# A fused attention and FFN kernel: row maxima by PSUM bank in a ring of four, weighted sums in bursts of two tiles

## What is computed

```python
# x: (8, 512, 1024) f32; mask = cond_2048: (8, 1024) of 0 and 1; 16 heads of 32 channels
Q, K, V = (einsum('oc,bct->bto', W, x) for W in (Wq, Wk, Wv))
att = einsum('bhqd,bhkd->bhqk', Q, K) / sqrt(32) + b
att = att * m + (1 - m) * -1e30
att = softmax(att)
y = einsum('bhqk,bhkd->bhqd', att, V)          # back to (8, 512, 1024)
absmax = max(|y|) over the last axis (1024); scale = max(absmax, 1e-7) / 127
q = clip(round(y / scale), -128, 127).astype(int8)
acc = einsum('bsk,nk->bsn', q, weight)          # int8 weight 1024 x 1024
out = x + (acc * scale * w_scale + bias).astype(float16)
```

## Time and profile before

| | us |
|---|---|
| median of 3 runs (lowest, highest) | 2414.74 (2414.34, 2416.75) |
| the profiled execution, its own time | 2414.74 |
| its span, first to last instruction | 2412.8 |
| TensorE busy | 2342.3 (97%) |
| GpSimd busy | 1725.1 (71%) |
| VectorE busy | 1561.4 (65%) |
| ScalarE busy | 1343.3 (56%) |

### The profile page before, as it was taken

How to read it: one execution, slowest core, us unless ns; L and a number is a source line. 1 busy time by engine, 2 the same in 40 slices (tenths; PEclk the granted TensorE clock), 3 DMA queues, 4 the chain that set the end, 5 groups by cost and what they waited for, 6 DMA issues and landing times.

```text
span 2412.8 us, 36511 instructions
## 1 busy us (share of the span) xinstructions
PE 2342.3 (97%) x11840; PEld 1320.4 (55%) x11872; DVE 1561.4 (65%) x1683; ACT 1343.3 (56%) x2536; POOL 1725.1 (71%) x740
## 2 busy tenths in 40 slices
PE   8999999999999999999999999999999999999996
PEld 7888888885444444444444444444444444444442
DVE  3311111147787777777787877777778777787771
ACT  3322222215666666666666666666666666666664
POOL 3322233324888888888888888888888888888887
PEclk9999999999999999999999999999999999999998
DMA  6645554467888888898988998888988888989971
GB/s 244 255 187 216 200 200 184 175 213 165 194 185 194 193 191 199 195 195 196 203 194 191 195 194 193 190 188 191 196 195 184 197 190 195 201 193 194 204 151 47
DMA packets 152569, 462.60 MB, mean 192 GB/s; under 512 B 15592, under 2 KB 51432, under 8 KB 128304
## 3 DMA queue, kind: packets, MB, share of 16 engines
q0 software_dynamic: 27216, 198.19, 42.9%
q10 hardware_dynamic: 48864, 129.19, 20.5%
q1 hardware_dynamic: 76416, 134.34, 15.5%
HBM read 161.51 MB, written 100.93 MB: 109 GB/s over the span
## 4 chain that ended last, share of the span: by engine, by line
PE 77%; DMA 10%; POOL 5%; issue 3%; ACT 2%; ACTq 1%; SPq 1%; DVE 1%; POOLq 0%; DVEq 0%
PE score L725 18%; PE pv L754 16%; PE ring L131 15%; PE ring L324 11%; PE score L324 9%; DMA q_stack<-max_lo 8%; PE ring L788 4%; POOL acc L1026 4%; PE pv L324 3%; PE ring L769 1%; ACT probs L836 1%; DMA k_stack<-bias_part 1%; ACTq L119 1%; DMA probs<-probs 1%; PE ring L779 1%
## 5 line engine op out<-in xcount | busy, mean ns | idle before, releaser
L836 ACT ACTIVATE probs<-score 128x512 f32<-128x512 f32 x2048 | 1076.8, 604 | 590.6 <-PE score L725 539.8
L140 DVE TENSOR_REDUCE neg_max<-ring 128x1 f32<-128x1024 f32 x1024 | 1210.8, 1220 | 260.3 <-PE ring L131 251.8
L725 PE MATMUL score<-q_stack,k_stack 100*128 100x512 f32 x2048 | 878.1, 430 | 36.4 <-DMA q_stack<-max_lo 21.1
L1026 POOL TENSOR_TENSOR acc<-acc,probs 128x2048 f32<-128x2048 f32 x189 | 876.8, 4639 | 21.5 <-DMA probs<-probs 12.9
L131 PE MATMUL ring<-k_stack,q_stack 98*128 98x512 f32 x2048 | 811.4, 396 | 2.8 <-DMA k_stack<-bias_part 1.8
L725 PEld LDWEIGHTS score<-q_stack,k_stack 100*128 100x128 f32 x2048 | 386.1, 189 | 530.1 <-ACT probs L836 370.9
L754 PE MATMUL pv<-probs,v_in 128*32 128x512 f32 x4096 | 546.3, 605 | 0.0
L131 PEld LDWEIGHTS ring<-k_stack,q_stack 98*128 98x128 f32 x2048 | 389.3, 190 | 73.4 <-DVE neg_max L140 6.8
L1026 POOL TENSOR_TENSOR acc<-probs 128x2048 f32<-128x2048 f32 x63 | 288.7, 4582 | 191.5 <-DMA probs<-probs 121.9
L526 POOL TENSOR_TENSOR q_stack<-x_raw,k_stack 128x1024 fp32r<-128x1024 f32 x28 | 67.7, 2455 | 292.2 <-ACT k_stack L402 292.2
L1010 POOL DMA_DIRECT2D probs<-probs x189 | 172.8, 914 | 52.2 <-PE pv L754 48.8
(11 more groups left out here) (101 smaller groups left out, 1950.0 us busy)
## 6 DMA issues: line engine op xcount, KB each, us to landing
probs<-probs POOLq DMA_DIRECT2D x189, 1024.0 KB, 9.1
q_stack<-qk_part ACTq DMA_DIRECT2D x183, 256.0 KB, 7.9
k_stack<-qk_part ACTq DMA_DIRECT2D x90, 512.0 KB
qk_part<-part_hi SPq DMA_DIRECT2D x64, 512.0 KB, 2.6
qk_part<-part_lo SPq DMA_DIRECT2D x64, 512.0 KB, 3.5
v_steps<-v_out SPq DMA_DIRECT2D x64, 256.0 KB, 2.2
v_out<-x ACTq DMA_DIRECT2D x32, 512.0 KB, 5.6
out<-v_out SPq DMA_DIRECT2D x64, 256.0 KB, 2.0
```

What stands on the lines that cost most here:

```text
L140: nc.vector.tensor_reduce(neg_max[:, pair // CHUNK, pair % CHUNK:pair % CHUNK + 1], ring[:, :], AX_X, ALU.max, negate=True).then_inc(neg_m ...
L725: pe.matmul(score[score_bank(t)][:, :], k_stack[par][0:ROWS, h, kt * P:(kt + 1) * P], q_stack[par][0:ROWS, half, h, :], start=True, stop=T ...
L836: nc.scalar.activation(probs[:, kt, h, :], score[score_bank(t)][:, :], ACT.Exp).then_inc(exp_done, 1)
L1026: nc.gpsimd.tensor_tensor(acc[:, half, :, :], first, probs[:, tile, :, :], ALU.add).then_inc(acc_done, 1)
```

## The change

The maxima are taken per PSUM bank: VectorE makes 64 maxima of 128x512 in a step, and the ring is four single banks. A new operation, `join_max`, takes the smaller of the two negated half maxima for a chunk, twice over, so that the transposed chunk holds both parts' rows and one DMA stores both. `weigh` runs for two tiles at t % 8 = 3. The extras move to t = 19 (transposed maxima), 27 (sums), 51 (transposed maxima), 55 (`turn_q`), 59 (sums and FFN); each takes one bank. ScalarE rounds in two operations of 128x1024. All loads of `attend` go from ScalarE's queue to SP's. GpSimd's pairs are tiles 0 to 1, 4 to 5 and 6 to 7, its additions 1 + 2, 3, 5, 7, and its order in a step is new; bias and residual come one step later. The last step has an order of its own: a fourth bank for scores once the maxima are done, the second half's sums by TensorE from five tiles and two pairs' results, VectorE and ScalarE sharing the rounding, and no extra pass. Cut to its core:

```diff
 RING = 8
-PAIRS_OF_TILES = ((0, 1), (2, 3), (6, 5))
-FIRST, ADDED = 4, (1, 3, 7, 5)
+PAIRS_OF_TILES = ((0, 1), (4, 5), (6, 7))
...
+OWN = 18
 EARLY = (UNITS - OWN) // 2
-SUMS_1, TURN_Q, FFN, SUMS_0 = 23, 47, 51, 55
-EXTRAS = (SUMS_1, TURN_Q, FFN, SUMS_0)
-USES = [use for t in range(1, UNITS, 2) for use in ((("max", t), ("extra", t)) if t in EXTRAS else (("max", t),))]
+HALVES = 2 * PAIRS
+BURST = 2 * GH
+RINGS = 4
+TURN_1, SUMS_1, TURN_0, TURN_Q, SUMS_0 = 19, 27, 51, 55, 59
+FFN, SKEW = SUMS_0, SUMS_1
+EXTRAS = {TURN_1: ("turn",), SUMS_1: ("sums",), TURN_0: ("turn",), TURN_Q: ("turn_q",),
+          SUMS_0: ("unused", "sums", "ffn0", "ffn1")}
...
+def reduce_max(nc, dve, bank, half_max, s, pair, half, rowmax_done, neg_max_done):
+    dve.wait_ge(rowmax_done, HALVES * s + 2 * pair + half + 1)
+    nc.vector.tensor_reduce(half_max[:, pair // CHUNK, pair % CHUNK, half:half + 1], bank[:, :],
                             AX_X, ALU.max, negate=True).then_inc(neg_max_done, 1)
...
+def join_max(nc, dve, half_max, neg_max, s, chunk, neg_max_done, joined):
+    dve.wait_ge(neg_max_done, HALVES * s + 2 * CHUNK * (chunk + 1))
+    nc.vector.tensor_reduce(neg_max[:, chunk, :].rearrange("p (d c) -> p d c", d=2),
+                            half_max[:, chunk, :, :].rearrange("p (o c) k -> p o c k", o=1).to_broadcast([P, 2, CHUNK, 2]),
+                            AX_X, ALU.min).then_inc(joined, 1)
...
+def store_max(sp, q_stack, max_parts, par, chunk, max_rows):
+    dst = q_stack[par][ROW_MAX:ROW_MAX + 2, chunk, :, :]
+    sp.dma_start(dst.bitcast(F32), max_parts[:, chunk, :].bitcast(F32)).then_inc(max_rows[chunk], 16)
...
+            def step(s, par, prev=True, ahead=True):
+                first = isinstance(s, int) and s == 0
+                second = not isinstance(s, int) or s >= 2
+                if ahead and not first:
+                    sp.wait_ge(score_done, UNITS * s)
+                    for k in range(3):
+                        load_k(sp, qk_d, k_stack, s + 1, 1 - par, k, k_loaded)
+                    for part in range(2):
+                        load_bias(sp, bias_d, k_stack, s + 1, 1 - par, part, k_loaded)
+                if second:
+                    store_out(s - 2, 0)
                 if ahead:
...
+                    if first:
+                        for i in range(2):
+                            sp.wait_ge(v_stored[i], 16 * B * TT // 2)
+                    wait(sp, pv_done, QH * TT * s)
+                    sp.dma_start(v_in[:, 1 - par, :, :], v_d[bass.ds(s + 1, 1)].rearrange("o p a c -> (o p) a c")).then_inc(v_loaded[1 - par], 16)
+                sp.wait_ge(max_lo_done, 2 * s + 2)
+                store_max(sp, q_stack, max_parts, par, 1, max_rows)
+                if ahead:
+                    for k in range(3):
+                        load_q(sp, qk_d, q_stack, s + 1, 1 - par, 1, k, q2_loaded)
+                if second:
+                    store_out(s - 2, 1)
+                    sp.wait_ge(out_stored, 32 * (s - 1))
+                if prev:
+                    sp.dma_start(res[:, :], x[bass.ds((s - 1) * P, P), :]).then_inc(res_loaded, 16)
+                if ahead:
                     sp.wait_ge(max_lo_done, 2 * s + 3)
...
+                    store_max(sp, q_stack, max_parts, 1 - par, 0, max_rows)
+                if not isinstance(s, int) or s + 2 < STEPS:
...
+                    for k in range(3):
+                        load_q(sp, qk_d, q_stack, s + 2, par, 0, k, q1_loaded)
             sp.wait_ge(proj_done, PROJECTED)
...
+            def step(s, par, prev=True, ahead=True):
                 for t in range(UNITS):
...
+                    scores(s, par, t)
+                    if has_max(t, ahead):
                         next_max(s, par, t)
                     if t == GH - 1 and prev:
...
+                        for kt in (QH * TT - 2, QH * TT - 1):
+                            weigh(s - 1, 1 - par, kt)
+                    if t % BURST == GH - 1 and t > GH:
+                        for kt in (t // GH - 2, t // GH - 1):
+                            weigh(s, par, kt)
+                    if t == TURN_1:
+                        turn_max(pe, take_ring(s, ("turn", t)), neg_max, ident, s, 1, joined, maxT_done)
+                    if t == SUMS_1 and prev:
+                        sum_rows(s - 1, 1, take_ring(s, ("sums", t)))
+                    if t == TURN_0 and ahead:
+                        turn_max(pe, take_ring(s, ("turn", t)), neg_max, ident, s + 1, 0, joined, maxT_done)
                     if t == TURN_Q and prev:
...
+                        turn_q(s - 1)
+                    if t == SUMS_0 and ahead:
+                        sum_rows(s, 0, take_ring(s, ("sums", t)))
                     if t == FFN and prev:
...
+                        ffn(s - 1)
+                    if not ahead and t == UNITS - 1:
+                        pe.wait_ge(prod_done, 2 * LAST - 1)
+                        last_sums = ring_of(("ffn0", FFN))
+                        for tile in (2, 3, 4, 5):
+                            sum_tile(tile, last_sums, start=tile == 2)
+                        for kt in (QH * TT - 2, QH * TT - 1):
+                            weigh(s, par, kt)
+                        sum_rows(s, 0, take_ring(s, ("sums", SUMS_0)))
+                        for tile in (6, 7, 1):
+                            sum_tile(tile, last_sums, stop=tile == 1)
...
+            def step(s, prev=True, ahead=True):
                 for t in range(UNITS):
...
+                    exps(s, t)
+                    if t == GH - 1 and prev:
                         take_y(s - 1, 1)
...
+                    if t == TURN_1:
+                        high_max(nc, act, ring_of(("turn", t)), max_parts, marks, s, 1, maxT_done, max_rows, max_hi_done)
+                    if t == UNITS // 2 + GH - 1:
                         take_y(s, 0)
...
+            def step(s, par, prev=True, ahead=True):
                 for t in range(UNITS):
...
+                    if has_max(t, ahead):
                         own, pair = max_of_slot(s, t)
...
+                        reduce_max(nc, dve, ring_of(("max", t)), half_max, own, pair, t % 2, rowmax_done, neg_max_done)
+                    if t == OWN - 1:
+                        join_max(nc, dve, half_max, neg_max, s, 1, neg_max_done, joined)
+                    if t == TURN_1 and prev:
+                        take_absmax(s - 1, 0)
+                        take_floor(s - 1)
+                    if t == TURN_1:
+                        low_max(nc, dve, ring_of(("turn", t)), max_parts, marks, s, 1, max_hi_done, max_lo_done)
                     if t == SUMS_1 and prev:
...
+                        recip(s - 1, 1, ring_of(("sums", t)))
                     if t == SUMS_1 + 4 and prev:
                         spread(s - 1, 1)
...
+                    if t == ROUND - 4 and prev:
                         take_absmax(s - 1, 1)
                         scales(s - 1)
+                    if t == OWN + 2 * CHUNK - 1 and ahead:
+                        join_max(nc, dve, half_max, neg_max, s + 1, 0, neg_max_done, joined)
+                    if t == TURN_0 and ahead:
+                        low_max(nc, dve, ring_of(("turn", t)), max_parts, marks, s + 1, 0, max_hi_done, max_lo_done)
                     if t == TURN_Q and prev:
...
+                        take_qT(s - 1)
+                    if t == SUMS_0 and ahead:
+                        recip(s, 0, ring_of(("sums", t)))
                     if t == FFN and prev:
                         for half in range(2):
...
+            def step(s, par, prev=True, ahead=True):
+                second = not isinstance(s, int) or s >= 2
+                if second:
+                    add_bias(s - 2, 0)
+                    add_residual(s - 2, 0)
+                if prev:
+                    begin_pair(s - 1, 1, 2)
+                    add(s - 1, 1, 2)
+                begin_pair(s, 0, 0)
                 if prev:
                     normalise(s - 1, 0)
...
+                    add(s - 1, 1, 3)
+                add(s, 0, 0)
+                begin_pair(s, 0, 1)
+                add(s, 0, 1)
                 if prev:
                     normalise(s - 1, 1)
...
+                if second:
+                    add_bias(s - 2, 1)
+                begin_pair(s, 0, 2)
+                add(s, 0, 2)
+                begin_pair(s, 1, 0)
+                if second:
+                    add_residual(s - 2, 1)
+                add(s, 0, 3)
+                if ahead:
+                    add(s, 1, 0)
                     begin_pair(s, 1, 1)
...
```

More of the change, by code:

```diff
@@ L125, in set_rows, with row_max @@
     nc.gpsimd.memset(q_stack[ROW_BIAS:ROWS, :, :, :].bitcast(F32), LIFT).then_inc(stack_set, 1)
-def row_max(pe, ring, q_stack, k_stack, par, pair, half, rowmax_done):
+def row_max(pe, bank, q_stack, k_stack, par, pair, half, rowmax_done):
     chunk, h, qt = pair // CHUNK, pair // GH % GH, pair % GH
[L131 to L134, removed]
@@ L378, in batch @@
```

(38 more changed lines are left out.)

406 lines of the change are left out of this document (170 added, 236 removed).

## The result

The forecast was 2320 us and faster. The change makes the kernel **slower: 2477.13 us** in the median of 4 runs (2471.56 to 2483.16) against 2414.54 (2413.28 to 2416.75) of the kernel before beside it, a ratio of 1.026 (95% interval 1.023 to 1.029).

What follows compares the result with a forecast made beforehand. The prediction took TensorE to set the pace, with GpSimd and VectorE close behind. It summed 557.2 + 31 steps x 54.3 + 78 = 2318.5 us of span, plus 1.9 outside, to 2320 us against 2414.74, range 2285 to 2380.

Steps and rivals of the forecast that it cites:

- about as before: Loads of the next step's keys: needed at t = 18, two units earlier, with no change expected and no size given.
- The pair rival: GpSimd's pair DMAs bind as landings stay at 9.1 or rise: step 55.0 to 56.5, 2342 to 2389 us, chance 0.26.
- four landings of 9.1: GpSimd's waits for pairs: 4 x 9.1 less 29.7 us of other work, added to 48.3, a step of 55.0.
- TensorE's work, 52.3: TensorE's new work in a step of `attend`, units, bursts, sums, `turn_q` and FFN together: 52.3 us.
- the late starts that I had summed: VectorE starting its maxima late after the sums at t = 27 and after the FFN: 0.5 and 0.8, 1.3 us a step.
- Maxima of 512 at 0.60: VectorE's maxima per bank: 0.60 us each in a row, 64 a step, VectorE fuller but not binding in the mean.
- the slow rival: VectorE binds if a short maximum costs 0.75 us: step 58.9, 2463 us, chance 0.07.
- Rows of the maxima, 0.3 a step: TensorE's waits for rows of the maxima: 1.0 us a step goes, 0.3 is put back.
- Sums that wait for GpSimd, 0.4: Sums at t = 27 and 59 wait for GpSimd's additions: 0.4 us a step.
- Last step and end, 78: The last step and what follows it: 78 us against 88.0 before, bounds 73 and 85.
- All waits hide: Rival for the step of `attend`: all waits hidden, step 53.0, 2280 us, chance 0.08.
- the 0.90 for faster: Chance that the whole kernel gets faster by over 0.2%: 0.50 + 0.26 + 0.08 + 0.08, less 0.02.

Runs made afterwards that it cites:

- a3: The changed kernel without the key and mask-row loads from step 1 on, so later steps score with old keys: 2278.15 us.
- c2: The changed kernel with the next step's keys needed at unit 22 instead of 18, transposed maxima moved to t = 23 and 54: 2458.01 us.
- a2: The changed kernel with GpSimd's pairs, additions and their order as before the change, all loads still on SP's queue: 2584.12 us.
- e1: The changed kernel without the pair of tiles 6 and 7 of the second half, tile 6's exponentials missing from the row sums: 2344.62 us.
- e2: The changed kernel without the load of v_in from step 2 on, so old values are weighed again: 2456.55 us.
- c1: The changed kernel with the v_in load and SP's store of the first half issued behind the query loads: 2448.78 us.
- d1: The kernel before the change with the next step's keys needed at unit 16 instead of 20, nothing else: 2517.61 us.

## Why the prediction was wrong, point by point

- **The step that failed:** "Keys are needed at t = 18, two units earlier, with all five loads at the step's start; about as before." It got no sum. My own terms give it: before, 20 units and five weighings lie ahead of the need, 20 x 0.467 + 5 x 1.18 = 15.2 us (15.7 measured); after, 18 units and two bursts, 8.4 + 4.1 = 12.5 (13.5 in the mean). A transfer of 15.4 us in the mean had lost two to three of them. A row of before for the landing of the keys was to be had, and I read landings only of stores, maxima and pairs. What the runs showed in place of "about as before": TensorE waits for the keys in 27 steps, 112.2 us in all, the longest 7.7, and the slow clock behind comes on top. All that the key loads cost, lateness and bytes together, is the 199 us between a3 and the changed kernel.
- **The pair rival** had the right mechanism and missed its first victim. I let loads stretch the pairs; the pairs also stretched a load, from 15.4 to 17.1 us in the mean of 30 steps. And it was priced too low: GpSimd's waits for pairs were 252.8 us, some 8.4 a step, where four landings of 9.1 less 29.7 made 6.7, and in c2, with the keys nearly in time, they lead the chain at 59.0 a step, where the rival had 55.0 to 56.5. The Trainium skill (DMA: Bandwidth & Descriptors, Queues, rings and completion order) has each engine go round-robin between the queues that it has work for, a packet at a time. The traces agree in so far as neither queue stands still for the other: while the keys load, q0 has 49 to 64% of the engines' time in the stretches shown (31% and 35% in a2 and e1, with fewer pairs) and the other queues the rest. That they take turns by the packet is not shown by any run here. By that rule I should have asked of every load beside a pair when it lands.
- **TensorE's work, 52.3:** right. Eight units with a burst take 5.82 us (scores at 1415.48 and 1421.30 in TensorE's timeline), less 8 x 0.467 that is 2.08 for the burst, forecast as 2.04 from the earlier trace rows; without key loads the whole step was 53.0, so all stalls together were 0.7 there, not 2.0. With them TensorE waited 1.2 us a step for single maxima (12.1 us in 10.5 steps, where I had 1.3). These waits come near unit 50, in steps where VectorE stood waiting for GpSimd's `y` (32.0 us, 11 times), so they hang on the pairs and not on the late starts that I had summed.
- **Maxima of 512 at 0.60** (bounds from the earlier trace rows): right. VectorE's timeline has:

```profile
1409.58 4.88 DVE L147 TENSOR_REDUCE half_max<-ring 128x1 f32<-128x512 f32 x8
```

  Eight starts fit in 4.88 with the last one's 0.68: (4.88 - 0.68) / 7 = 0.60. So the slow rival (VectorE binds from 0.73 on) did not come true; the time ended on its side, by another mechanism.
- **Rows of the maxima, 0.3 a step:** 1.4 us in the whole run. **Sums that wait for GpSimd, 0.4:** 3.1 us in 10.5 steps, 0.3.
- **Pairs, four landings of 9.1:** their median is 9.2 with keys (the earlier trace rows had 9.1) and 8.0 in a3, whose step was 53.0. The longest is 15.7, not 11.5. That they don't bind is shown only for the kernel without the keys' bytes.
- **Last step and end, 78:** 75.
- **"All waits hide" (step 53.0, 2280)** is what the kernel does without the key loads: a3 ran in 2278. Part of this match is luck, since the rival left the loads in.
- The range's lower part and the 0.90 for faster rested on terms for the engines that were right; what was missing was the transfers' share, the keys above all. That the rest would have come to 54.3 with the keys in time is not shown: no run has the same bytes and no key waits. The engines' mean share, "0.93 of 54.3", stood in the text, and I used it for pairs alone.

## What to carry to other kernels

List every transfer's landing against the moment it is needed, also those that show no wait: a load that arrives just in time has hardly a row among the waits, and any edit that shortens the work in front of it turns it into the bound. The DMA engines' 0.89 in the mean hid stretches here in which they were full, and in these a load's duration was its own bytes plus those of the pairs beside it. Work taken off the path in front of a deadline is worth nothing until the deadline moves with it; and moving it may not be enough, as in c2, where the same full engines then held up the next transfer in line.

## What the runs showed that I had not expected

- The price of a wait on TensorE is more than its length: after the waits of 3.5 to 7.7 us the granted clock stood at 0.50 for some 3 to 10 us. The Trainium skill (TensorE: Matmul & The Clock Gate, What's actually happening) has a cold level of 1.2 GHz and a warm one of 2.4; the row of 0.50 and a burst of 3.57 us instead of 1.85 fit that.
- Full engines moved 200 to 228 GB/s in the stretches read here, loads and accumulating pairs together.
- A transfer's neighbours matter by place: 0.5 MB behind it on the same queue cost it nothing to speak of (e2), query loads ahead on the same queue did delay it (a2), and a MB of pairs on another queue went with 4.7 us more (c1), 3.0 where a pair was taken away (e1).
- The landing of the keys was steady in d1, an edit of the old kernel (14.6 to 16.0), and wide in the changed one (12.3 to 21.2). GpSimd issues each pair when its last one and `pv` allow, so how much of the pairs falls beside the keys changes from step to step. What would hold them apart without loss was not tried.
